# Expert stage: y stores, bias loads and weight-centring transfers moved from SyncE's queue to ScalarE's, token-order tables by matmul

## The chip, the cores and the metric

One Trainium2 chip, one program on its 8 cores, each core with one of the 8 batch rows of x (2048 tokens of 1024 values). Nothing is exchanged between cores. The metric is the device time of the slowest core in microseconds. Each core has TensorE (PE), VectorE (DVE), ScalarE (ACT), GpSimd (POOL) and SyncE (SP, which only issues transfers); 16 DMA engines per core carry what SP, ACT or POOL issue.

## The reference

Two layers, each with an attention-like block and a feed-forward block, every block followed by `x = layernorm(x + block(x))`:

```
L0_attn: state = tanh(state @ A.T + u_t @ B.T) + sp_t ; out = (state @ C.T) @ Wo.T + bo     (a scan)
L0_ffn:  8 experts, the 2 best per token:
         logits = x @ gate_w.T + gate_b ; probs = softmax(logits) ; top 2
         out = sum over the 2 of  prob_e * ( relu(x @ w1[e] + b1[e]) @ w2[e] + b2[e] )
         w1[e]: 1024 x 4096, w2[e]: 4096 x 1024
L1_attn: q, k, v = x @ Wq.T, x @ Wk.T, x @ Wv.T ; 16 heads of 64 ; layernorm of q and k per head ; causal attention ; @ Wu.T
L1_ffn:  token shift, r = sigmoid(xr @ W_r.T), k = relu(xk @ W_k.T)^2, out = r * (k @ W_v.T)
```

## The kernel before, in words

The program is written as five instruction lists, one per engine. Helpers (`MM`, `AC`, `DV`, `GP`, `DMA`, `E`) append an instruction with the semaphore values that it waits for, and `run` issues each list in order. So **each engine's order is the order of the Python code**, a wait at the head of an engine's list holds everything behind it, and in the profile nearly every instruction has the line of `run`, L1431 (the gathers have L1416). Groups are told apart by tile names.

Stages: the scan (0 to about 215 us); routing, in which each token's normed row `x1b` is scattered in bf16 to the rows `xg_d` (`xgs`) of its two experts by POOL's indirect transfers (`scatter`); the experts; the gathering of the two results of each token (`fetch`, `combine`); queries, keys and values; attention; the last feed-forward block.

**Routing.** `route` computes for each of 16 tiles of 128 rows the target row of each row's two copies, `posU`, and `ends` computes the gate values, `gate`. Both are in the scan's order: row 32k+s is position k of the 64-token run s. After the experts the tokens are wanted in their own order, so `posN` and `gateN` hold the same numbers with the rows permuted: partition 64h+k of tile i is position k of run 2i+h. Before, they are made by storing `posU` and `gate` to DRAM (`po_d`, `ga_d`: `to_table`) and reading them back with another access pattern (`of_table`), rows of 8 bytes each.

**Experts.** Each of the 8 experts has a fixed capacity of 640 rows. `load_xg(e)` is one transposing transfer (`dma_start_transpose`) of 640 x 1024 bf16 from `xg_d` into `xgT[e % 2]`. `mlp` then runs:

- first product: 32 blocks `hb` of 128 hidden units, each 8 x 2 matmuls of 128x320 into PSUM banks 0 and 1 or 2 and 3; ACT's Relu with bias turns each block into `hT`.
- second product: 5 tiles `s` of 128 rows, each 32 x 2 matmuls of 128x512 into banks 4 and 5 (even s) or 6 and 7 (odd s); DVE adds the bias row `b2r` into `yst[s % 2]`, which frees the two banks; then `yst` is stored to `yb_d` (`ybs`). A tile s needs the banks that tile s-2 used, so TensorE can run two tiles ahead of DVE's sum.

Weights come by POOL's queue in 32 casting transfers per expert (f32 in DRAM, bf16 in SBUF): `load_w1(e+1, c)` when the first product of expert e has used chunk c, `load_w2(e+1, c)` when the last tile of its second product has.

The loop over experts also hides a job for layer 1: the centring of Wq and Wk in 32 pieces, 4 per expert. `center_load(j)` loads a piece into the single buffer `wqf`, `center_run(j)` lets DVE take the mean of each 64 columns off (`wsum`, `wqc`) and stores it to `wc_d` (`wcs`).

Before, all of these are in SP's queue, in this order for expert e: the transposing load of e+1 (its wait is the end of the first product of e-1); during the first product at blocks 0, 8, 16, 24 a `center_load` and at 4, 12, 20, 28 a `center_run` with its store; at block 1 `load_b2(e)` (which waits for the last sum of e-1); then the five y stores. The loads of the centred weights `WqS`, `WkS`, of `cb2` and of `x1c` follow behind the last expert.

Of the kernel before, what the change touches and what calls it, by code (L numbers as in the profile page):

```python
# [13 lines left out]
T = 2048  # L14
D = 1024
NE = 8
# [16 lines left out]
def build():  # L33
    nc = bass.Bass("TRN2", target_bir_lowering=False)

    def din(name, shape, dtype=F32):
        return nc.dram_tensor(name, list(shape), dtype, kind="ExternalInput").ap()
# [8 lines left out]
    bo_d = din("bo", [1, D])  # L46
    cf_d = din("cf", [128, 310])
    cg_d = din("cg", [128, 80])
    cb_d = din("cb", [128, 640], BF16)
    lnrow_d = din("lnrow", [1, 256])  # L50
    w1_d = din("w1", [NE, 16, 128, 2048])
# [12 lines left out]
    rc_d = scratch("rcs", [16, T], F32)  # L64
    lo_d = scratch("los", [1, T], F32)
    ao_d = scratch("aos", [8, 128, T], BF16)
    po_d = scratch("pos", [T, 2], U32)
    ga_d = scratch("gas", [T, 2], F32)
    bl_d = scratch("bls", [2, D], BF16)

    base = (nc.sbuf_base + 63) & ~63
# [57 lines left out]
    bib = place("bib", [128, 512], BF16, OY + 6912)  # L129
    b3 = place("b3", [3, D], BF16, OB)  # L130
    xgE = [place(f"xgE{i}", [8, 512], F32, (OB + 2048, OF + 26624)[i]) for i in range(2)]
    sz = place("sz", [128, NTILE], F32, OB + 7424)
    WiF = place("WiF", [128, D], F32, O1)
    WsF = place("WsF", [128, 8, 128], F32, O1 + 4096)
# [87 lines left out]
    def V(s):  # L222
        return (side[0] + s, cnt.get(side[0] + s, 0))
# [34 lines left out]
    t_bo = DMA("sync", "lbo", bo1[0], bo_d)  # L258
    DMA("sync", "lc", cf, cf_d)
    DMA("sync", "lc", cg, cg_d)  # L260
    t_lc = V("lc")
    gwT, boT, I8 = cg[:, 0:64].rearrange("p (c e) -> p c e", c=8), cg[:, 64:72], cg[0:8, 72:80]
    DMA("sync", "lw", BTf, BT_d)
# [194 lines left out]
    def post(S, nx):  # L458
# [94 lines left out]
        def route(nt):  # L553

            i0, n = 4 * nt, 4
            bank = 6 + nt % 2
            ts = slice(i0, i0 + n)
            L, o0, o1, M = LG[:, ts], ohs[0][:, ts], ohs[1][:, ts], Mall[:, ts]
            a, b, c, d = (tm[j][:, 0:n] for j in range(4))
            mx = tm[4][:, 0:n]  # L560
            v1, v2, vA, vB = (tv[j][:, 0:n] for j in range(4))

            def ex(x):
                return x.unsqueeze(2).broadcast_to([128, n, NE])

            def al(x):
                return x.unsqueeze(1).broadcast_to([128, n, NE])

            t = DV("tensor_tensor", a, ex(mv[:, ts, 0]), al(SgB), ALU.mult, w=(st["sg"], S.get("rt")))
            t = DV("tensor_tensor", b, ps[:, bank, 0:8 * n].rearrange("p (i e) -> p i e", e=NE), a,  # L570
                   ALU.subtract, w=(t, S["lg", nt]))
            t = DV("tensor_tensor", c, b, ex(rs[:, ts]), ALU.mult, w=(t, S["rs", i0 + n - 1]))
            t = DV("tensor_tensor", L, c, al(gbr), ALU.add, w=(t,))
            for i in range(n):
                t = DV("max", mx[:, i, :], L[:, i, :], w=(t,))
            DV("tensor_copy", MX[:, ts], mx[:, :, 0], w=(t,))
            t = DV("tensor_tensor", a, L, mx[:, :, 0:1].broadcast_to([128, n, NE]), ALU.is_equal)
            t = DV("tensor_tensor", b, a, al(rev8), ALU.mult, w=(t,))
            t = DV("tensor_reduce", v1, b, AX.X, ALU.max, w=(t,))
            t = DV("tensor_tensor", c, al(rev8), ex(v1), ALU.is_equal, w=(t,))  # L580
            t = DV("scalar_tensor_tensor", d, c, -1e30, L, ALU.mult, ALU.add, w=(t,))
            t = DV("tensor_tensor", a, d, mx[:, :, 1:2].broadcast_to([128, n, NE]), ALU.is_equal, w=(t,))
            t = DV("tensor_tensor", b, a, al(rev8), ALU.mult, w=(t,))
            t = DV("tensor_reduce", v2, b, AX.X, ALU.max, w=(t,))
            DV("tensor_tensor", vA, v1, v2, ALU.max, w=(t,))
            t = DV("tensor_tensor", vB, v1, v2, ALU.min)
            DV("tensor_tensor", o0, al(rev8), ex(vA), ALU.is_equal, w=(t,))
            t = DV("tensor_tensor", o1, al(rev8), ex(vB), ALU.is_equal)
            t = DV("tensor_tensor", M, o0, o1, ALU.add, w=(t,))
            for i in range(i0, i0 + n):  # L590
                t = DV("tensor_tensor", Mc[:, i + 1, :], Mc[:, i, :], Mall[:, i, :], ALU.add, w=(t,))
            S["mc"] = t
            r = ps[:, bank, 256:256 + 8 * n]
            MM(r, Lst, M.rearrange("p i e -> p (i e)"), start=True, stop=False, w=(t, t_cb))
            t = MM(r, ones_b, Mc[:, ts].rearrange("p i e -> p (i e)"), start=False, stop=True, inc=True)
            r = r.rearrange("p (i e) -> p i e", e=NE)
            t0 = DV("tensor_tensor", a, r, al(eoff), ALU.add, w=(t,))
            t = S["rf", nt] = DV("scalar_tensor_tensor", b, r, float(CAP), al(kadd), ALU.is_ge, ALU.mult)
            t = DV("tensor_tensor", c, a, b, ALU.add, w=(t,))
            for k, o in enumerate((o0, o1)):  # L600
                t = DV("tensor_tensor", a, c, o, ALU.mult, w=(t,))
                t = DV("tensor_reduce", (v1, v2)[k], a, AX.X, ALU.add, w=(t,))
                t = DV("tensor_copy", posU[:, ts, k], (v1, v2)[k], w=(t,))
            S["rt"] = S["pos"] = t

        def scatter(i):
# [7 lines left out]
        def ends():  # L614
# [10 lines left out]
            for k in range(2):  # L625
                t1 = DV("tensor_tensor", ge[2], ge[1], ohs[k], ALU.mult, w=(t,))
                t1 = DV("tensor_reduce", gs[0], ge[2], AX.X, ALU.add, w=(t1,))
                t = S["gate"] = DV("tensor_tensor", gate[:, :, k], gs[0], gs[1], ALU.mult, w=(t1,))

        return load_x, tile_z, tile_all, tile_n, gate_x, gate_y, route, scatter, ends  # L630

# [106 lines left out]
    t_scat = tuple(st["scg", g] for g in range(4))  # L738
    t_x1all = tuple(st["x1s", i] for i in range(10, NTILE))
    t_vscan, t_pscan, t_gscan, t_ascan = V("v"), V("p"), V("g"), V("a")  # L740
    t_gate, t_fl = st["gate"], st["fl"]

    tk = {("a", 0): t_vscan, ("a", 2): t_ascan, ("y", 4): t_gate}
# [1 line left out]
    def mlp(e, row0, nst, xsrc, tx, tk, t_w1, t_w2):  # L746
# [16 lines left out]
        for s in range(nst):  # L763
            bk = 4 + 2 * (s % 2)
            for kb in range(32):
# [5 lines left out]
                if s == nst - 1 and kb % 2 == 1:  # L771
# [3 lines left out]
            tk["y", bk] = DV("tensor_tensor", yb, ps[:, bk:bk + 2, :], b2r, ALU.add,  # L775
                             w=(t, tk["b2", e], tk.get(("ys", s % 2))))
            tk["yv", e] = tk["y", bk]
            tk["ys", s % 2] = DMA("sync", f"sy{s % 2}", yb_d[row0 + s * 128:row0 + (s + 1) * 128, :], yb,
                                  w=(tk["y", bk],))
            yield ("y", s)  # L780

    def load_b2(e, w=()):
        tk["b2", e] = DMA("sync", "b2", b2r, b2_d[e:e + 1, :].partition_broadcast(128), w=w)

    x1p = x1_d.rearrange("(s k) d -> k s d", k=NSEG)

# [7 lines left out]
    for c in range(8, 16):  # L794
# [2 lines left out]
    tk["ys", 0] = t_zf  # L797

    to_table = [(d.rearrange("(i p) c -> p i c", p=128), o) for d, o in ((po_d, posU), (ga_d, gate))]  # L800
    of_table = [(o[64 * h:64 * h + 64], d.rearrange("(s i h) c -> h s i c", i=NTILE, h=2)[h]) for h in range(2)
                for d, o in ((po_d, posN), (ga_d, gateN))]

    with only_if(flag[0:1, 0:1], t_fl, "x"):
        X = chain()
        for o, i in to_table + of_table:
            X("sync", "dma_start", out=o, in_=i)
        rest = xg_d[MAIN:ROWS, :].rearrange("(a p r) d -> a p (r d)", p=128, r=2)
        fill = hT[:, 0:4, :].rearrange("p a b -> p (a b)")[:, 0:2048]  # L810
        X("vector", "memset", fill, 0.0)
# [34 lines left out]
    def center_load(j):  # L846
        m, k, h = j // 16, j // 2 % 8, j % 2
        src = (WqT_d, WkT_d)[m]
        st["wl", j] = DMA("sync", "wl", wqf, src[k * 128:(k + 1) * 128, h * 512:(h + 1) * 512],
                          w=(st.get(("wc", j - 1)), t_vscan, t_gate, t_pscan))  # L850

    def center_run(j):
# [4 lines left out]
        t = DV("tensor_tensor", wqc.rearrange("p (h s) -> p h s", s=64), v,  # L857
               wsum.unsqueeze(2).broadcast_to([128, 8, 64]), ALU.subtract, w=(t, st.get(("ws", j - 1))))
        st["wc", j] = t
        st["ws", j] = DMA("sync", "ws", wc_d[m, k * 128:(k + 1) * 128, h * 512:(h + 1) * 512], wqc, w=(t,))  # L860

    for e in range(NE):
        if e + 1 < NE:
            load_xg(e + 1, w=(tk.get(("m1", e - 1, 31)),))
        for ev, j in mlp(e, e * CAP, CAP // 128, xgT[e % 2], tk["xg", e], tk, t_w1, t_w2):
            if ev == "m2" and e == 0 and j == 0:
                for o, i in to_table:
                    DMA("sync", "tab", o, i, w=(t_gate,))
                t_tab = V("tab")
            if ev == "m1" and e == 1 and j == 8:  # L870
                for o, i in of_table:
                    t_pos = DMA("sync", "tab", o, i, w=(t_tab,))
            if ev == "m1" and j % 8 == 0:
                center_load(4 * e + j // 8)
            if ev == "m1" and j % 8 == 4:
                center_run(4 * e + j // 8)
            if ev == "m1" and j == 1 and e > 0:
                load_b2(e, w=(tk["yv", e - 1],))
            if ev == "m1" and j % 2 == 1 and e + 1 < NE:
                load_w1(e + 1, j // 2, w=(tk["m1", e, j],))  # L880
            if ev == "m2" and e + 1 < NE:
                load_w2(e + 1, j, w=(tk["m2", e, j],))
# [577 lines left out]
def _prep(i):  # L1460
# [18 lines left out]
    for j, k in enumerate(("qln_w", "qln_b", "kln_w", "kln_b")):  # L1479
# [7 lines left out]
    cf[:, 294:302] = MAIN - CAP + e * (T - 2 * CAP)  # L1487
    cf[:, 302:310] = A("L0_ffn_gate_b")
    d["cf"] = cf
    d["cg"] = C(np.concatenate([A("L0_ffn_gate_w").reshape(8, 8, 128).transpose(2, 1, 0).reshape(128, 64),  # L1490
                                A("L0_attn_bo").reshape(8, 128).T, np.eye(128, 8, dtype=np.float32)], 1))
    d["lnrow"] = C(np.concatenate([A("L1_attn_" + k) for k in ("qln_w", "qln_b", "kln_w", "kln_b")]).reshape(1, 256))
# [32 lines left out]
```

How the kernel before makes its waits and increments, by code:

```python
    def run(eng, lst):  # L1402
        for method, args, kw, need, s, n in lst:
            plain = method in HELD or method in ("wait_", "if_", "gather_")
            for sn, v in need if plain else need[:-1]:
                eng.wait_ge(sems[sn], v)
            if method == "wait_":
                continue
            if method == "gather_":
# [4 lines left out]
                        for c in calls:  # L1414
                            call = {k: v for k, v in c.items() if k != "sem"}
                            eng.indirect_dma_start(**call).then_inc(sems[c["sem"][0]], 16)
                continue
# [5 lines left out]
            if method == "held_":  # L1423
                out, weights, rhs = args
                ins = eng.add_instruction(mybir.InstMatmult(
                    name=nc.get_next_instruction_name(), engine=mybir.EngineType.PE, start_tensor_calc=False,
                    stop_tensor_calc=True, tile_size=(128, 128), tile_position=(0, 0), ldweights=False,
                    bass_skip_group_check=True, ins=(eng.lower_ap(rhs), eng.lower_ap(weights)),
                    outs=(eng.lower_ap(out),)))
            else:
                ins = getattr(eng, method)(*args, **kw)
            if need and not plain:
                ins._wait_ge(sems[need[-1][0]], need[-1][1])
            if s is not None:
                ins.then_inc(sems[s], n)
```

## Time and profile before

| | |
|---|---|
| median of 3 runs | 2644.66 us (2635.55 to 2655.49) |
| the profiled execution: its own time | 2658.42 us |
| its span on core 6, the slowest | 2656.8 us |
| spans of the 8 cores | 2628.6 to 2656.8 us |
| granted TensorE clock, mean of each core | 0.883 to 0.889 |
| TensorE busy | 1989.0 us (75%) |
| DMA | 304.33 MB moved, mean 115 GB/s |

The span runs from the first to the last instruction of a core; the time beside it is 1.6 us longer. A granted clock of 1.00 is 2.4 GHz, 0.50 is 1.2 GHz. SPq is SP as issuer of transfers: its duration is that of the issue, not of the transfer. Times of rows are in us from the span's start unless marked ns.

### The profile page before, as it was taken

To read this page: it belongs to the slowest core of one execution; us is meant where nothing else is said; L and a number is where in the kernel's file an instruction comes from. 1 tells how busy PE (TensorE), PEld (TensorE's weight loads), DVE (VectorE), ACT (ScalarE), POOL (GpSimd) and SP (SyncE) were. 2 spreads that over 40 slices of the span, in tenths; PEclk is the share of its full clock that TensorE was granted. 3 is DMA by queue.
4 is the path that set the end of the run, shared out by engine and by line. 5 is a ranking of instruction groups with operands and counts; after the bars stand their busy time and mean duration, and the time that the engine had idled before them with its cause. 6 is when DMAs were issued, how large, how long until landed. Compare 5 with 4: busy or idle time off the path is not lost.

```text
span 2656.8 us, 25477 instructions; the slowest of 8 cores (2628.6 to 2656.8 us)
## 1 busy us (share of the span) xinstructions
PE 1989.0 (75%) x10425; PEld 999.1 (38%) x10537; DVE 692.7 (26%) x1350; ACT 808.8 (30%) x1159; POOL 439.7 (17%) x484
## 2 busy tenths in 40 slices
PE   5653939919969599696996992778788778566766
PEld 2112615605527255272562741333233223232332
DVE  4541010010010100101001102663344344355454
ACT  2222201201203012030120300456678778333222
POOL 1124101001011010010100002210123232112133
PEclk9666969959979799797997996999989999788988
DMA  9677976977939769397693826750001411611100
GB/s 273 226 184 178 167 138 85 128 132 125 164 93 169 139 117 170 89 168 146 116 168 89 155 64 195 212 164 9 2 17 25 86 27 25 131 36 56 40 32 40
DMA packets 143494, 304.33 MB, mean 115 GB/s; under 512 B 63984, under 2 KB 69873, under 8 KB 141300
## 3 DMA queue, kind: packets, MB, share of 16 engines
q0 software_dynamic: 49296, 169.90, 37.9%
q1 hardware_dynamic: 94052, 132.51, 18.3%
q8 instruction: 89, 1.46, 0.2%
q14 instruction: 57, 0.47, 0.1%
HBM read 367.08 MB, written 69.37 MB: 164 GB/s over the span
## 4 chain that ended last, share of the span: by engine, by line
SPq 28%; PE 26%; issue 12%; DVE 12%; ACT 11%; DMA 7%; POOL 4%; DVEq 0%; POOLq 0%; ACTq 0%; another core or an unknown queue 0%
SPq L1431 28%; PE ps L1431 26%; ACT PT L1431 5%; DMA wqf<-WqT 3%; ACT rsd L1431 2%; DVE PT L1431 2%; DMA wqf<-WkT 2%; POOL x3f L1431 1%; DVE lstf L1431 1%; DVE wsum L1431 1%; DMA sumC<-stg 1%; ACT sq L1431 1%; DVE xk L1431 1%; DVE rf L1431 1%; DVE xt L1431 1%
## 5 line engine op out<-in xcount | busy, mean ns | idle before, releaser
L1431 PE MATMUL ps<-W,hT 128*128 128x512 bf16 x2504 | 566.1, 387 | 233.9 <-DVE yst L1431 231.0
L1431 PE MATMUL ps<-xgT,W 128*128 128x320 bf16 x4096 | 559.9, 300 | 30.6 <-DMA xgT<-xgs 30.1
L1431 ACT ACTIVATE hT<-ps,cf 128x640 bf16<-128x640 f32 x256 | 203.0, 793 | 1081.9 <-PE ps L1431 1081.9
L1431 PEld LDWEIGHTS ps<-xgT,W 128*128 128x128 bf16 x4096 | 401.4, 98 | 188.7 <-issue 30.2
L1431 PEld LDWEIGHTS ps<-W,hT 128*128 128x128 bf16 x2560 | 253.6, 99 | 545.1 <-DVE yst L1431 234.4
L1431 POOL DMA_DIRECT2D W<-w x256 | 135.6, 537 | 1103.4 <-PE ps L1431 1049.1
L1431 ACT ACTIVATE PT<-ps 128x1024 bf16<-128x1024 f32 (+7 forms) x384 | 272.0, 793 | 82.2 <-PE ps L1431 79.3
L1431 DVE TENSOR_REDUCE wsum<-wqf 128x8 f32<-128x512 f32 x32 | 21.9, 686 | 921.6 <-DMA wqf<-WqT 535.1
L1431 PE MATMUL ps<-PT,Vg 128*128 128x512 bf16 (+3 forms) x628 | 191.9, 365 | 58.1 <-DVE PT L1431 56.6
L1431 PE MATMUL ps<-qz,KT 128*128 128x512 bf16 (+3 forms) x627 | 186.9, 364 | 19.1 <-POOL qz L1431 12.4
L1431 DVE TENSOR_TENSOR PT<-PT,cb 128x128 bf16<-128x128 bf16 x256 | 111.6, 456 | 177.3 <-ACT PT L1431 174.4
L1431 DVE TENSOR_TENSOR yst<-ps,b2r 128x1024 f32<-128x1024 f32 x40 | 48.3, 1222 | 362.8 <-PE ps L1431 362.8
L1431 PEld LDWEIGHTS ps<-PT,Vg 128*128 128x128 bf16 x640 | 65.1, 102 | 143.1 <-DVE PT L1431 92.2
L1431 POOL TENSOR_TENSOR aoT<-stg,recB 64x2048 bf16<-64x2048 f32 x15 | 67.6, 4506 | 194.8 <-DMA recB<-rcs 194.8
L1431 PEld LDWEIGHTS ps<-qz,KT 128*128 128x128 bf16 x640 | 51.1, 101 | 110.5 <-ACT PT L1431 76.9
L1431 PE MATMUL ps<-Wu,aoT 128*128 128x512 bf16 x249 | 67.3, 429 | 30.4 <-DVE aoT L1431 18.6
L1431 PE MATMUL ps<-WvS,x2T 128*128 128x512 bf16 x249 | 64.8, 416 | 32.7 <-ACT x2T L1431 32.4
L1431 PE MATMUL ps<-xk,Wkf 128*128 128x512 bf16 x250 | 60.9, 402 | 14.4 <-DVE xk L1431 14.0
L1431 PE MATMUL ps<-Wr,xr 128*128 128x512 bf16 x249 | 58.9, 387 | 14.8 <-DVE xr L1431 8.7
L1431 PE MATMUL ps<-x2T,WqS 128*128 128x512 bf16 x250 | 62.8, 383 | 0.4 <-issue 0.2
L1431 POOL TENSOR_TENSOR x3f<-x3f,rf 128x1024 f32<-128x1024 f32 x16 | 37.5, 2342 | 140.7 <-DVE rf L1431 140.7
L1431 PE MATMUL ps<-x2T,WkS 128*128 128x512 bf16 x251 | 60.2, 379 | 0.7 <-ACT sq L1431 0.5
(208 smaller groups left out, 1578.6 us busy)
## 6 DMA issues: line engine op xcount, KB each, us to landing
W<-w POOLq DMA_DIRECT2D x256, 512.0 KB, 39.3
ybs<-yst SPq DMA_DIRECT2D x40, 512.0 KB, 2.8
xgs<-zero SPq DMA_DIRECT2D x20, 512.0 KB, 17.1
xTf<-xT SPq DMA_DIRECT2D x8, 1024.0 KB, 18.1
xt<-x SPq DMA_DIRECT2D x16, 512.0 KB, 8.7
x1s<-xt SPq DMA_DIRECT2D x16, 512.0 KB, 5.0
x1c<-x1s SPq DMA_DIRECT2D x32, 256.0 KB, 7.7
x2s<-x1c SPq DMA_DIRECT2D x16, 512.0 KB, 2.9
```

Source lines behind the costliest of these rows:

```text
L1431: ins = getattr(eng, method)(*args, **kw)
```

## The change

In the expert loop SP's queue keeps only the transposing loads. The y stores, the bias loads and both transfers of each centring piece go to ACT's queue. The centring is no longer spread over the first product: at the event behind tile s of the second product comes `center_run` of the piece before (s > 0), then `center_load` of the next (s < 4), and behind tile 4 the bias load of the next expert. The tables `posN` and `gateN` are no longer sent through DRAM: `posU`'s values are kept in f32 (`posF`), DVE multiplies them and `gate` with a mask into `perm` (four operations, 128x128 each), four f32 matmuls with a constant `peye` (16 columns) put them in token order, and three small DVE operations write `posN` and `gateN`. A constant `cp` of 128 x 24 f32 is loaded at the start of SP's queue.

```diff
+    t_cp = DMA("sync", "lcp", cp, cp_d)
...
-                t = DV("tensor_reduce", (v1, v2)[k], a, AX.X, ALU.add, w=(t,))
-                t = DV("tensor_copy", posU[:, ts, k], (v1, v2)[k], w=(t,))
+                t = DV("tensor_reduce", posF[:, ts, k], a, AX.X, ALU.add, w=(t,))
+                t = DV("tensor_copy", posU[:, ts, k], posF[:, ts, k], w=(t,))
...
+            for v, src in enumerate((posF[:, :, 0], posF[:, :, 1], gate[:, :, 0], gate[:, :, 1])):
+                t = DV("tensor_tensor", perm[:, v].rearrange("p (h i r) -> p h i r", h=2, r=4),
+                       pmask.rearrange("p (h r) -> p h r", h=2).unsqueeze(2).broadcast_to([128, 2, NTILE, 4]),
+                       src.unsqueeze(1).unsqueeze(3).broadcast_to([128, 2, NTILE, 4]), ALU.mult, w=(t, t_cp))
+            for v in range(4):
+                t1 = MM(ps[:, 7, 192 + 16 * v:208 + 16 * v], perm[:, v], peye, start=True, stop=True, w=(t,),
+                        inc=(v == 3))
+            r = ps[:, 7, 192:256].rearrange("p (v i) -> p i v", v=4)
+            t = DV("tensor_scalar", ge[2][:, :, 0:2], r[:, :, 0:2], 0.25, None, ALU.add, w=(t1,))
+            t = DV("tensor_copy", posN, ge[2][:, :, 0:2], w=(t,))
+            S["posn"] = DV("tensor_copy", gateN, r[:, :, 2:4], w=(t,))
...
-            tk["ys", s % 2] = DMA("sync", f"sy{s % 2}", yb_d[row0 + s * 128:row0 + (s + 1) * 128, :], yb,
+            tk["ys", s % 2] = DMA("scalar", f"sy{s % 2}", yb_d[row0 + s * 128:row0 + (s + 1) * 128, :], yb,
...
-        tk["b2", e] = DMA("sync", "b2", b2r, b2_d[e:e + 1, :].partition_broadcast(128), w=w)
+        tk["b2", e] = DMA("scalar", "b2", b2r, b2_d[e:e + 1, :].partition_broadcast(128), w=w)
...
-        st["wl", j] = DMA("sync", "wl", wqf, src[k * 128:(k + 1) * 128, h * 512:(h + 1) * 512],
+        st["wl", j] = DMA("scalar", "wl", wqf, src[k * 128:(k + 1) * 128, h * 512:(h + 1) * 512],
...
-        st["ws", j] = DMA("sync", "ws", wc_d[m, k * 128:(k + 1) * 128, h * 512:(h + 1) * 512], wqc, w=(t,))
+        st["ws", j] = DMA("scalar", "ws", wc_d[m, k * 128:(k + 1) * 128, h * 512:(h + 1) * 512], wqc, w=(t,))
...
-            if ev == "m2" and e == 0 and j == 0:
-                for o, i in to_table:
-                    DMA("sync", "tab", o, i, w=(t_gate,))
-                t_tab = V("tab")
-            if ev == "m1" and e == 1 and j == 8:
-                for o, i in of_table:
-                    t_pos = DMA("sync", "tab", o, i, w=(t_tab,))
-            if ev == "m1" and j % 8 == 0:
-                center_load(4 * e + j // 8)
-            if ev == "m1" and j % 8 == 4:
-                center_run(4 * e + j // 8)
-            if ev == "m1" and j == 1 and e > 0:
-                load_b2(e, w=(tk["yv", e - 1],))
+            if ev == "y":
+                if j > 0:
+                    center_run(4 * e + j - 1)
+                if j < 4:
+                    center_load(4 * e + j)
+                elif e + 1 < NE:
+                    load_b2(e + 1, w=(tk["yv", e],))
```

## Rows read from the trace of the kernel before

**Rows 1.** The page: shares of the chain that ended last, by line.
```profile
SPq L1431 28%; PE ps L1431 26%; ACT PT L1431 5%; DMA wqf<-WqT 3%; ACT rsd L1431 2%; DVE PT L1431 2%; DMA wqf<-WkT 2%; POOL x3f L1431 1%; DVE lstf L1431 1%; DVE wsum L1431 1%; DMA sumC<-stg 1%; ACT sq L1431 1%; DVE xk L1431 1%; DVE rf L1431 1%; DVE xt L1431 1%
```

**Rows 2.** The page: the second product; busy, mean ns, idle before, releaser.
```profile
L1431 PE MATMUL ps<-W,hT 128*128 128x512 bf16 x2504 | 566.1, 387 | 233.9 <-DVE yst L1431 231.0
```

**Rows 3.** Timeline of PE, 380 to 1620 us: start, length, idle before and releaser.
```profile
391.02 44.01 PE L1431 MATMUL ps<-W,hT 128*128 128x512 bf16 x188 [46.08 <-DVE yst L1431]
...
586.44 43.58 PE L1431 MATMUL ps<-W,hT 128*128 128x512 bf16 x188 [54.24 <-DVE yst L1431]
629.85 69.71 PE L1431 MATMUL ps<-xgT,W 128*128 128x320 bf16 x512
...
753.66 43.59 PE L1431 MATMUL ps<-W,hT 128*128 128x512 bf16 x188 [26.47 <-DVE yst L1431]
...
1535.15 69.02 PE L1431 MATMUL ps<-W,hT 128*128 128x512 bf16 x313
```

**Rows 4.** Timeline of SP's queue, 230 to 800 us: start, length of the issue.
```profile
236.69 6.00 SPq L1431 DMA_TRANSPOSE xgT<-xgs  x1
...
423.46 18.32 SPq L1431 DMA_DIRECT2D gas<-gate  x1
441.88 58.00 SPq L1431 DMA_DIRECT2D ybs<-yst  x1
500.01 61.41 SPq L1431 DMA_TRANSPOSE xgT<-xgs  x1
...
631.83 98.63 SPq L1431 DMA_TRANSPOSE xgT<-xgs  x1
...
731.14 0.67 SPq L1431 DMA_DIRECT2D b2r<-b  x1
...
737.41 0.33 SPq L1431 DMA_DIRECT2D wcs<-wqc  x1
```

**Rows 5.** Timeline of DVE, 590 to 800 us.
```profile
630.12 1.23 DVE L1431 TENSOR_TENSOR yst<-ps,b2r 128x1024 f32<-128x1024 f32 x1 [12.59 <-PE ps L1431]
...
735.65 0.69 DVE L1431 TENSOR_REDUCE wsum<-wqf 128x8 f32<-128x512 f32 x1 [104.30 <-DMA wqf<-WqT]
...
736.64 0.69 DVE L1431 TENSOR_TENSOR wqc<-wqf,wsum 128x512 bf16<-128x512 f32 x1
...
752.39 2.35 DVE L1431 TENSOR_TENSOR yst<-ps,b2r 128x1024 f32<-128x1024 f32 x2
```

**Rows 6.** Busy time by stretch: PE, PEld, DVE, ACT, POOL, granted clock, DMA share, GB/s.
```profile
753.00:757.00 4.00, 3.34 (x8) 1.19 (x9) 1.73 (x2) 0.00 (x0) 0.00 (x0) 0.50 0.73 290
...
629.00:797.00 168.00, 141.16 (x830) 82.19 (x836) 12.13 (x17) 25.41 (x32) 16.71 (x32) 0.92 0.79 137
...
1421.00:1605.00 184.00, 182.33 (x1013) 100.74 (x1024) 16.83 (x22) 25.38 (x32) 10.12 (x18) 0.98 0.47 95
```

**Rows 7.** DMA, 700 to 797 us: busy tenths in 40 slices, transfers by median us to landing.
```profile
DMA  9999999999999991314050650000031000058999
...
wqf<-WqT SPq DMA_DIRECT2D x4, 256.0 KB, 2.9
...
wcs<-wqc SPq DMA_DIRECT2D x4, 128.0 KB, 1.8
```

**Rows 8.** The same of 629 to 700 us: weights and the transposing load in flight.
```profile
ybs<-yst SPq DMA_DIRECT2D x1, 512.0 KB, 9.2
```

**Rows 9.** Timeline from the last expert to layer 1, all engines.
```profile
1606.06 0.38 SPq L1431 DMA_DIRECT2D WqS<-wcs  x1
...
1635.68 1.28 DVE L1431 SCALAR_TENSOR_TENSOR x1c<-yA,gateN,x1c 128x1024 f32<-128x1024 f32 x1 [30.18 <-DMA x1c<-x1s]
```

**Rows 10.** Timeline of the start, and of the end of routing.
```profile
1.89 0.42 SPq L1431 DMA_DIRECT2D cg<-cg  x1
...
219.23 0.18 DVE L1431 TENSOR_TENSOR gate<-gs,gs 128x16 f32<-128x16 f32 x1
...
233.45 0.96 POOL L1431 DMA_INDIRECT xgs<-x1b,posU  x1 [0.30 <-issue]
```

More of the change, by code:

```diff
@@ L48, in build @@
     cg_d = din("cg", [128, 80])
+    cp_d = din("cp", [128, 24])
     cb_d = din("cb", [128, 640], BF16)
@@ L66, in build @@
     ao_d = scratch("aos", [8, 128, T], BF16)
-    po_d = scratch("pos", [T, 2], U32)
-    ga_d = scratch("gas", [T, 2], F32)
     bl_d = scratch("bls", [2, D], BF16)
@@ L131, in build @@
     xgE = [place(f"xgE{i}", [8, 512], F32, (OB + 2048, OF + 26624)[i]) for i in range(2)]
+    cp = place("cp", [128, 24], F32, OB + 7488)
+    posF = place("posF", [128, NTILE, 2], F32, OB + 7584)
+    perm = place("perm", [128, 4, 128], F32, OF + 4096)
     sz = place("sz", [128, NTILE], F32, OB + 7424)
@@ L260, in build @@
     DMA("sync", "lc", cg, cg_d)
+    t_cp = DMA("sync", "lcp", cp, cp_d)
+    pmask, peye = cp[:, 0:8], cp[:, 8:24]
     t_lc = V("lc")
@@ L740, in build @@
     t_vscan, t_pscan, t_gscan, t_ascan = V("v"), V("p"), V("g"), V("a")
-    t_gate, t_fl = st["gate"], st["fl"]
+    t_gate, t_fl, t_pos = st["gate"], st["fl"], st["posn"]
     tk = {("a", 0): t_vscan, ("a", 2): t_ascan, ("y", 4): t_gate}
@@ L797, in build @@
     tk["ys", 0] = t_zf
-    to_table = [(d.rearrange("(i p) c -> p i c", p=128), o) for d, o in ((po_d, posU), (ga_d, gate))]
-    of_table = [(o[64 * h:64 * h + 64], d.rearrange("(s i h) c -> h s i c", i=NTILE, h=2)[h]) for h in range(2)
-                for d, o in ((po_d, posN), (ga_d, gateN))]
     with only_if(flag[0:1, 0:1], t_fl, "x"):
         X = chain()
-        for o, i in to_table + of_table:
-            X("sync", "dma_start", out=o, in_=i)
         rest = xg_d[MAIN:ROWS, :].rearrange("(a p r) d -> a p (r d)", p=128, r=2)
@@ L1489, in _prep @@
     d["cf"] = cf
+    q = np.arange(128)[:, None]
+    j = np.arange(16)[None]
+    d["cp"] = C(np.concatenate([(q % 2 == j[:, :8] // 4) & (q // 32 == j[:, :8] % 4), q % 32 // 2 == j], 1), np.float32)
     d["cg"] = C(np.concatenate([A("L0_ffn_gate_w").reshape(8, 8, 128).transpose(2, 1, 0).reshape(128, 64),
```

## The prediction

> **What bounds the kernel now.** I read the page's chain first: 28% of the span is SP's queue as issuer [rows 1], an engine that computes nothing. The page's group of the second product says whom it holds: TensorE is idle for 231.0 us before these matmuls, all put down to DVE's `yst` [rows 2]. PE's timeline shows where. The second product of an expert runs two of its five tiles, then stands still, then runs the other three: 46.08 us in expert 0, 54.24 in expert 1, 26.47 in expert 2 [rows 3], and four more of 24.63 to 26.95 in experts 3 to 6. Expert 7 has none: its 320 matmuls take 69.02 us in one piece [rows 3].
>
> SP's timeline gives the reason. The transposing load for expert 3 is issued at 631.83, behind the last y store of expert 1, and its issue alone takes 98.63 us; behind it in the same queue stand a centring piece and the bias row of expert 2, issued at 731.14 [rows 4]. DVE, in order too, waited 104.30 us for the first piece, then did four pieces with a load's latency between each, and only at 752.39 came to the two sums that free the PSUM banks [rows 5]; PE resumes at 753.66. In expert 1 the same queue was blocked once more, by the tables: storing `gate` in rows of 8 bytes took 18.32 us to issue and the y store behind it 58.00, so that the transposing load began at 500.01 [rows 4].
>
> Each stall costs something after its end too. The granted clock is 0.50 (1.2 GHz) in the 4 us after the restart, following 26 us without matmuls [rows 6]. Three tiles without a stall are 3/5 of 69.02 = 41.4 us; the restarted three of expert 2 plus start of the next product are 43.4 us (I take start to start). Over the seven restarts these pieces add to 305.4 us from PE's timeline, of which the first, second and third have their rows [rows 3], against 7 x 41.4 = 289.9: 15.5 us.
>
> **The stalls removed.** With the transposing loads alone in SP's queue, nothing that DVE's sums need stands behind them. Removed: 231.0 + 15.5 = 246.5 us. Check from the other side: from the start of expert 0's second product (317.4) to the end of expert 7's (1604.2) are 1286.8 us; eight second products of 69.02 and seven first ones of 69.76 are 1040.5; the difference is 246.3.
>
> **What is late next.** Three things could take the place of the wait.
>
> The transposing load. That of e+1 may now be issued when the first product of e-1 ends, and is needed 209 us later; its longest issue so far is 98.63 us, so it is covered twice. It should also be shorter: the first was issued in 6.00 us, before the weights started [rows 4]. Expert 0 is special: its load for expert 1 is issued at 249 and landed about 370 (121 us, the longest of the eight); the first product of expert 1 will now begin at 317.4 + 69 = 386.4. That leaves 16 us.
>
> The weights. The period of an expert falls from 167 us to 69.7 + 69.0 = 139 us, and the mean DMA share in it is 0.79 of 168 us [rows 6], which is 133 us of full DMA time. So DMA will be at 95%. It still fits: the burst begins with the last tile (616.9 for this period), and the row of slices falls from 9 to 1 at about 741 [rows 7], after 124 us, with everything that was queued moved; it includes the transposing load, whose bytes do not grow. The stall lies in the slack behind that and takes it from 44 us to 17. What the burst brings last is wanted a further product later, so a few us of lateness cost nothing; only a mean over 139 us would. I put 0 here, at most 8 us in each of 6 periods (50).
>
> ACT's queue. ACT now has the waits. In the second product it has no eviction to do, so a store that waits for DVE there delays nobody. At the end it does: behind the last store stand the store of the centring piece and the next bias load, and behind these the Relu of block 0 of the next expert, which PE needs before block 2, 4.36 us after its start. Counted from PE's start at 629.85: the sum ends at 631.35, the piece's DVE work takes 1.68 (735.65 to the end of `wqc` at 737.33), so its store can be issued at 633.1, with 0.33 for it and 0.43 to 0.67 for the bias row, by SP's rows [rows 4, 5]; then the Relu, 0.79, ends at 634.9 and PE, which wanted it at 634.2, starts at about 635.0. That is 0.8 us, times 7 experts: **+5.6 us**. No row has ACT issuing a transfer; if it takes up to 1.3 us each instead of 0.4, three of them add 2.7 us per expert. So 4 to 25 us, and I stay near the lower end because SP's direct rows are the nearest.
>
> **The transfers themselves.** They meet weights and a transposing load now. A y store landed after 9.2 us in that company [rows 8]; a piece's load took 2.9 [rows 7]. With two `yst` buffers a store has some 26 us, and a piece's load some 11 us before DVE comes to it after the next sum (tiles come every 13.8 us). Even at 9.2 both are in time: 0. The bias row has 80 us.
>
> **The end of the experts.** Before, `WqS` was issued at 1606.06, right behind the last store, and the first `x1c` came behind it; DVE waited for that until 1635.68 [rows 9]. `WqS` needs the store of piece 31, which now is issued only after the last sum: sum ends 1605.5, DVE 1.7, issue 0.4, landing 1.8 [rows 7], so 1609.3. **+3.2 us**, taken in full since the whole chain behind moves with it; 0 to 4.
>
> **The tables.** Routing ends for DVE at 219.23; POOL's last scatter starts at 233.45 and the transposing load waits for it [rows 10]. Four operations of 0.3 us (128x128 f32, as that on `ge`), four f32 matmuls under 0.6 us, three small ones with hand-overs are some 4 us, beside POOL's 14: 0. If that cover were gone they would cost these 4. The extra constant is one more issue ahead of the loads of x: **+0.4 us** [rows 10].
>
> **The sum.** 246.5 - 5.6 - 3.2 - 0.4 = 237.3 us less. Against the profiled execution's own time, 2658.4, that gives 2421; it lay 13.8 us above the median of the runs shown, so against the median 2644.66 - 237.3 = **2407 us**. The seven other cores had 217.5 to 229.9 us of these waits, so the slowest core may gain a little less or be another; 10 us for that.
>
> **A rule that speaks against it.** The rows say that an issue can take 98.63 us when the queue is backed up [rows 4]. The Trainium skill, DMA: Bandwidth & Descriptors, section Issuing engines are not separate DMA queues, holds that all issuers share the same 16 engines and that several of them save only the sequencer's time, "usually small relative to the DMA itself". By it the gain would be some tenths of a us per store and the time unchanged; here the sequencer's time is what TensorE waits for, so I give it to the rival below that gains nothing.
>
> **The rivals.**
>
> A. ACT's stores are held up while SP issues a transposing load, for instance in something that both share; in the steady state that load then competes with weights only until some 40 us into the second product and ends there, just when the third sum wants its buffer, so it costs almost nothing. In experts 0 and 1 it does cost: the load for expert 2 follows at 346 right behind the one for expert 1 and lasts some 97 us, into expert 0's fifth tile at 373: about 75 us. Time 2480. For it: 58.00 us for one y store behind an 8-byte one [rows 4] shows that a queue can back up. Against: it was its own queue. 9%.
>
> B. The other side. As A, but the load keeps its 98 us in every expert, from the end of the first product. The third sum waits for the first store, PE stops at the fifth tile, 55 us into the product, until 98 plus some 5 us of landing and sum: 48 us, plus 2.2 of half clock, seven times 351 us in place of the 246.5. Time 2407 + 351 = 2758. It decides from a hold of 82 us on: 82 + 5 - 55 is a stall of 32 us, which with its 2.2 eats the whole 237.3 in seven experts. Against: nothing but weights slowed that load, and these have drained 124 us after the burst's start, which is 40 us into the second product. 4%.
>
> C. The weights become the bound: 5 to 10 us more in six periods, 2440 to 2465. For: 95% DMA. 8%.
>
> D. Nothing is gained since another wait takes over in full (a centring piece that lands late in front of each sum): about 2645. Pieces take 2.9 us alone, so it would need five times that under load. 3%.
>
> E. Unbroken work costs clock. Every 1% less over the 1110 us of the stage is 11 us; from a mean of 0.82 on the gain is gone. Against: 184 us with one short gap ran at 0.98 [rows 6]. The Trainium skill, TensorE: Matmul & The Clock Gate, Part 1, names a limiter that holds a die at 13/16 under dense matmuls on three or more cores; no row shows that here, with eight cores dense. By its figure, as an estimate, 256 us come back: 2663. 4%.
>
> **Chances.** My forecast 72%, A 9, B 4, C 8, D 3, E 4. Below it there is only the spread of the runs, 10 us, and a smaller cost at ACT: 2385. Above, C lies inside and A is the edge: 2485. A measurement here tells about 1% (26 us) from no change. Faster by over 1%: forecast, A and C, 89%, and half of E, 91%. Within 1%: D and half of E, 5%. Slower: B, 4%.
>
> **What would show it.** In the profile after: second products of 320 matmuls in one piece of 69 us, expert period 139 to 140 us; no PE wait on `yst`; a wait of 0.8 us on `hT` in front of block 2 of each expert; transposing issues well under 98 us from expert 3 on; DMA share about 0.95 in an expert; DVE's wait for `x1c` ending some 245 us earlier than 1635.68. I am wrong if ACT's issues of y stores are longer than 1 us, if POOL's weights or the first product wait on `W` or `xgT`, or if the granted clock of 400 to 1300 us is under 0.98.

## The result and the profile after

The changed kernel takes 2511.18 us (median of 4 runs; 2642.99 for the kernel before beside it). The ratio is **0.9473**, interval 0.9422 to 0.9523: faster, but by 139 us where 237 were forecast, and outside the range of 2385 to 2485 that I gave. Here and below, a run in which the cores of one die ran at a lower clock (of the four here, that of 2656 us) is left out of the ratio but not of the median, which is why the ratio isn't quite the quotient of the two medians. In the profiled execution (2509.64 us) the cores are no longer alike: their spans run from 2422.3 to 2508.0 us.

The page of the slowest core, core 7: the two products; the columns are those of [rows 2]:

```profile
L1434 PE MATMUL ps<-xgT,W 128*128 128x320 bf16 x4096 | 570.1, 303 | 118.1 <-ACT hT L1434 95.7
L1434 PE MATMUL ps<-W,hT 128*128 128x512 bf16 x2560 | 553.8, 379 | 0.0
```

The 231.0 us of idle time in front of the second product [rows 2] are 0.0. In their place stand 95.7 us in front of the first product, released by ACT's `hT`. PE's timeline on the same core, to be held against [rows 3]:

```profile
315.20 69.23 PE L1434 MATMUL ps<-W,hT 128*128 128x512 bf16 x320
384.26 4.51 PE L1434 MATMUL ps<-xgT,W 128*128 128x320 bf16 x32
468.15 67.43 PE L1434 MATMUL ps<-xgT,W 128*128 128x320 bf16 x480 [79.37 <-ACT hT L1434]
535.42 69.23 PE L1434 MATMUL ps<-W,hT 128*128 128x512 bf16 x320
604.48 4.51 PE L1434 MATMUL ps<-xgT,W 128*128 128x320 bf16 x32
609.79 65.37 PE L1434 MATMUL ps<-xgT,W 128*128 128x320 bf16 x480 [0.80 <-ACT hT L1434]
...
1174.64 4.51 PE L1434 MATMUL ps<-xgT,W 128*128 128x320 bf16 x32
1184.20 67.80 PE L1434 MATMUL ps<-xgT,W 128*128 128x320 bf16 x480 [5.05 <-ACT hT L1434]
```

Each second product runs in one piece. But the first product now stops after 32 matmuls, which are two blocks, and waits for the first Relu: 79.37 us in expert 1, then 0.80, 3.34, 2.62, 3.23, 5.05 and 1.34. The 480 matmuls behind take up to 67.80 us instead of 65.37 when the wait was long, the half clock again (9.5 us over the seven). The stage from expert 0's second product to expert 7's end lasts 1461.2 - 315.2 = 1146.0 us; 1286.8 before, 1040.5 without any wait.

What ACT did in these 79 us, in its own timeline (ACTq is ACT as issuer of transfers):

```profile
384.76 0.33 ACTq L1434 DMA_DIRECT2D wcs<-wqc  x1
385.11 0.45 ACTq L1434 DMA_DIRECT2D wqf<-WqT  x1
386.18 0.33 ACTq L1434 DMA_DIRECT2D ybs<-yst  x1
466.44 0.33 ACTq L1434 DMA_DIRECT2D wcs<-wqc  x1
466.80 0.45 ACTq L1434 DMA_DIRECT2D b2r<-b  x1
467.30 1.48 ACT L1434 ACTIVATE hT<-ps,cf 128x640 bf16<-128x640 f32 x2 [151.10 <-DVE wqc L1434]
```

And DVE:

```profile
464.68 0.69 DVE L1434 TENSOR_REDUCE wsum<-wqf 128x8 f32<-128x512 f32 x1 [78.86 <-DMA wqf<-WqT]
```

So the chain is: the load of the fourth centring piece, issued at 385.11, lands at 464.6, 79.5 us later; DVE waits for it; ACT waits for DVE with the piece's store at the head of its queue; the first Relu stands behind. The issues themselves are as short as SP's, 0.33 to 0.45 us.

The DMA view says what else was in flight. First 329 to 384 us, then 441 to 466 us of the same core; columns: packets, MB, share of 16 engines' time. q0 carries the weights, q1 what SP issues (here only transposing loads), q10 what ACT issues:

```profile
q0 software_dynamic: 1910, 6.96, 74.8%
q10 hardware_dynamic: 1278, 3.08, 18.5%
q1 hardware_dynamic: 2024, 0.51, 11.2%
```

```profile
q1 hardware_dynamic: 1066, 0.27, 136.5%
q0 software_dynamic: 104, 0.38, 8.4%
q10 hardware_dynamic: 64, 0.15, 3.4%
```

In the first stretch one packet of the transposing load takes 0.112 x 16 x 55 us / 2024 = 0.05 us. In the second it takes 1.365 x 16 x 25 / 1066 = 0.51 us, ten times as long, although the weights are nearly through; hardly anything else moves, ACT's packets included. But these are only the last 25 of the 79 us. In 408 to 440 us, with the piece's load issued and PE standing, q10 moves nothing at all:

```profile
q0 software_dynamic: 1351, 4.90, 81.1%
q1 hardware_dynamic: 1913, 0.49, 35.2%
```

Here weights run at 4.90 MB in 32 us, 153 GB/s, and a transposing packet takes 0.352 x 16 x 32 / 1913 = 0.09 us. So the slow packets are how the wait ends and not what it is made of; what holds ACT's packets in the 32 us before them the trace doesn't show. The transposing load in flight is that for expert 2: an issue of 115.80 us and 143.1 us to landing.

```profile
L1434 SPq DMA_TRANSPOSE xgT<-xgs x1: 115796/115796/115796, 337.6 to 337.6; - x1
...
DMA to landing us min/median/max: 143.1/143.1/143.1
```

The wait at expert 1 is 69.0, 39.2, 5.6, 57.6, 26.5, 8.4, 7.8 and 79.4 us on cores 0 to 7. Three cores (2, 5 and 6) wait 5.6 to 8.4 us only, and their spans, 2430.3, 2422.3 and 2440.8 us, are within 20 us of the 2421 of my sum. Core 4 waits 26.5 us although its transposing packets take no more than 0.05 us then (380 to 411 us: 1070 packets, 10.1%).

In the later experts the same chain is shorter. ACT at expert 5 of core 7:

```profile
1121.38 0.45 ACTq L1434 DMA_DIRECT2D wqf<-WkT  x1
1134.77 0.33 ACTq L1434 DMA_DIRECT2D ybs<-yst  x1
1153.87 0.33 ACTq L1434 DMA_DIRECT2D wcs<-wqc  x1
...
1182.33 0.33 ACTq L1434 DMA_DIRECT2D wcs<-wqc  x1
1182.68 0.62 ACTq L1434 DMA_DIRECT2D b2r<-b  x1
1183.35 1.48 ACT L1434 ACTIVATE hT<-ps,cf 128x640 bf16<-128x640 f32 x2 [76.78 <-issue]
```

The first piece's load, issued at 1121.38, holds its store back to 1153.87, 32 us; the other three catch up, but the fourth is stored at 1182.33, when PE had wanted the Relu at 1179.0.

### The profile page after: what moved, and what is told of

The parts are those of the page before. It is cut to its first block, busy times and chain, and to the rows that moved or that the text cites. A ratio compares the mean times of both kernels' runs of the same rounds, so it can differ in the third digit from the quotient of the medians.

```text
span 2508.0 us, 25623 instructions; the slowest of 8 cores (2422.3 to 2508.0 us)
## 1 busy us (share of the span) xinstructions
PE 1992.9 (79%) x10564; PEld 999.9 (40%) x10545; DVE 700.5 (28%) x1357; ACT 807.5 (32%) x1159; POOL 439.5 (18%) x484
## 4 chain that ended last, share of the span: by engine, by line
PE 51%; DVE 11%; ACT 11%; issue 9%; DMA 8%; POOL 4%; another core or an unknown queue 3%; SPq 0%; ACTq 0%; POOLq 0%; DVEq 0%
PE ps L1434 50%; ACT PT L1434 5%; DMA wqf<-WkT 3%; DMA wqf<-WqT 3%; DVE PT L1434 3%; ACT rsd L1434 3%; POOL x3f L1434 2%; DVE lstf L1434 1%; ACT sq L1434 1%; DVE xk L1434 1%; DVE rf L1434 1%; DVE xt L1434 1%; DMA xTf<-xT 1%; DVE lsmf L1434 1%
## 5 line engine op out<-in xcount | busy, mean ns | idle before, releaser
L1434 PE MATMUL ps<-xgT,W 128*128 128x320 bf16 x4096 | 570.1, 303 | 118.1 <-ACT hT L1434 95.7
L1434 PE MATMUL ps<-W,hT 128*128 128x512 bf16 x2560 | 553.8, 379 | 0.0
```

What stands on the lines that cost most here:

```text
L1434: ins = getattr(eng, method)(*args, **kw)
```

## The experiments

Where expert 1's wait is called long below, it is over 20 us. **Theory A**: the transposing load for expert 2, in flight beside ACT's transfers, holds them. **Theory B**: DMA is overloaded by weights at that place. Beside both: the fourth centring piece, ahead of the first Relu, is what turns a late transfer into idle TensorE. All ratios are against the kernel before on the same chip.

**1. The transposing loads one expert later.**

```diff
-        if e + 1 < NE:
-            load_xg(e + 1, w=(tk.get(("m1", e - 1, 31)),))
+        if e == 0:
+            load_xg(1)
...
+            if ev == "m1" and j == 31 and 0 < e < NE - 1:
+                load_xg(e + 1, w=(tk["m1", e, 31],))
```

> The changed kernel with the transposing loads of experts 2 to 7 issued one expert later (at the end of the first product of the expert before, not of the one before that), so that expert 0's second product has only the load for expert 1 beside it. Theory A (the ACT queue's transfers are held by the transposing load for expert 2, which starts right behind the one for expert 1 while weights are queued): TensorE's wait on hT at the start of expert 1 (5.6 to 79.4 us by core) falls below 10 us on every core, time 2425 to 2450. Theory B (DMA is simply overloaded by weights there): the wait stays at 40 us or more on the slowest cores, time 2490 to 2515.

Measured: 2465.73 us, ratio 0.9252 (0.9192 to 0.9312). The wait at expert 1 is 3.5 to 12.4 us over the eight cores. That is 0.022 of the time, 58 us of 2643, gained by moving one transfer. The worst waits are a little above the 10 us expected, and on four cores (0, 2, 5 and 6) waits of 2 to 5 us stay from expert 3 on. PE on core 0:

```profile
405.48 68.23 PE L1436 MATMUL ps<-xgT,W 128*128 128x320 bf16 x480 [10.67 <-ACT hT L1436]
548.36 65.37 PE L1436 MATMUL ps<-xgT,W 128*128 128x320 bf16 x480 [1.23 <-ACT hT L1436]
```

**2. The fourth piece later.** Its `center_run` at block 30 of the next expert's first product.

```diff
-                if j > 0:
+                if 0 < j < 4 or (j == 4 and e == NE - 1):
                     center_run(4 * e + j - 1)
...
+            if ev == "m1" and j == 30 and e > 0:
+                center_run(4 * e - 1)
```

> The changed kernel with the fourth centring piece of each expert worked on and stored at block 30 of the next expert's first product, so that between the last tile and the first Relu ACT has only a y store and the bias load. If the wait is that of ACT for DVE and of DVE for the piece's load: the wait on hT falls to 0 to 1 us in every expert, all cores, time 2415 to 2435. If ACT's own issues are what is held up: the wait of 79 us stays on the slowest core, time about 2510.

Measured: 2483.01 us, 0.9288 (0.9213 to 0.9363). Five cores show no wait on `hT` in any expert, with spans of 2403.5 to 2416.0 us. On the other three the slow stretch comes at other places: core 1 waits 82.51 us at expert 2, and on cores 3 and 4 PE stands still for 31.4 and 10.2 us inside expert 1's first product, with no releaser shown, and then waits on `W` some seven times for 0.8 to 2.6 us. Core 1:

```profile
615.53 4.71 PE L1436 MATMUL ps<-xgT,W 128*128 128x320 bf16 x24 [82.51 <-ACT hT L1436]
```

In expert 1's second product core 3 stands for another 22.8 us and core 4 for 8.3 us, and on core 1 a piece's load took 91.5 us to land. The five cores without a wait show that the fourth piece is what PE waits for in the changed kernel; the other three, that taking it out of the way doesn't take away what holds the transfers, it only moves the victim. A miss of both sizes expected.

**3. Each half alone.** `tables_alone` is the kernel before with the tables by matmul; `queues_alone` is the changed kernel with the tables through DRAM, whose diff is the table part of the change taken back.

> The kernel before with the tables by matmul and nothing else of the change. Expert 1's stall falls from 54.2 to that of the other experts, 26.5, and no other changes: 28 us less, time about 2615. Rival: the time in which the table stores delayed the transposing load is filled by it, no gain, 2643.

Measured: 2633.07 us, 0.985 (0.9758 to 0.9941), 40 us less with an interval of 16 to 65; the 28 expected lie inside. Expert 1's stall falls to that of the others, as expected; PE on core 4:

```profile
390.94 43.55 PE L1435 MATMUL ps<-W,hT 128*128 128x512 bf16 x188 [46.27 <-DVE yst L1435]
557.81 22.37 PE L1435 MATMUL ps<-W,hT 128*128 128x512 bf16 x91 [26.15 <-DVE yst L1435]
```

> The changed kernel with the tables through DRAM as before, in SP's queue. The table stores now stand between the transposing loads for experts 1 and 2. Theory A: what is in flight beside ACT's transfers at the end of expert 0 is then the store of the tables in 8 byte rows; if these hold ACT's transfers as the transposing load does, the wait at expert 1 is 40 to 80 us again, time 2500; if only a transposing load does it, the wait is under 10 us and the time 2440. Theory B: as the changed kernel, 2510.

Measured: 2558.78 us, 0.9555 (0.9472 to 0.9638), the time of neither theory. The waits at expert 1 are 9.6 to 20.0 us, but a new one comes that neither theory had: the table stores delay the transposing load for expert 2 until PE wants it. Core 0:

```profile
607.51 6.27 PE L1432 MATMUL ps<-xgT,W 128*128 128x320 bf16 x32 [72.19 <-DMA xgT<-xgs]
```

On cores 3, 4 and 7 there are also waits of 21.9 to 28.7 us on `hT` or `yst` in expert 2. By themselves the queues give 0.045 and the tables 0.015 of the time, together 0.053: most of the gain is the queues' part.

**4. Is it the transposing, the small packets, or the bytes?** `load_plain` loads the same bytes without transposing; `load_small` cuts them into as many pieces of 256 bytes as the transposing load has. The edit of `load_small`; that of `load_plain` has one piece of 10 KB per partition instead:

```diff
-        tk["xg", e] = E("sync", "dma_start_transpose", out=xgT[e % 2], in_=xg_d[e * CAP:(e + 1) * CAP, :],
+        tk["xg", e] = E("sync", "dma_start", out=xgT[e % 2].rearrange("p c (a d) -> p c a d", a=5),
+                        in_=xg_d[e * CAP:(e + 1) * CAP, :].rearrange("(a p) (c d) -> p c a d", p=128, c=8),
```

> The changed kernel with plain loads of the same bytes in place of the transposing ones (xgT then holds the rows in another order, so the experts compute on other numbers; all else is the same). Theory A (the transposing load holds the others): waits on hT under 3 us everywhere, time 0.915 of before. Theory B (too much DMA): waits of 40 to 80 us stay at expert 1 on the slowest cores, 0.947.

Measured: 2455.68 us, 0.921 (0.9134 to 0.9286). The wait at expert 1 is 4.9 to 10.2 us, in later experts 0.4 to 4.8.

> As load_plain, but the plain load is cut into 5120 pieces of 256 bytes per expert, the packet size and number of the transposing one. If small packets that take turns with weights are what fills the queues: the same slow stretch as in the changed kernel, waits of 40 to 80 us on the slowest cores. If it is the transposing itself: as load_plain.

Measured: 2461.99 us, 0.9234 (0.9158 to 0.931). The wait at expert 1 is 4.0 to 11.4 us. The worst core of each, 7 and 4:

```profile
397.19 68.07 PE L1435 MATMUL ps<-xgT,W 128*128 128x320 bf16 x480 [10.22 <-ACT hT L1435]
```

```profile
404.30 67.75 PE L1435 MATMUL ps<-xgT,W 128*128 128x320 bf16 x480 [11.43 <-ACT hT L1435]
```

No core of the two profiles has a long wait, though the bytes are the same: theory B falls. Small packets alone weren't seen to make one either. The two kernels also separate issue from landing. The issue of the load for expert 2 took 0.3 us plain, 0.6 us in small pieces and 37 to 133 us transposing; it landed after some 12 us plain, 138 to 145 us on six cores and 63 to 64 on two in small pieces, and 71 to 148 us transposing. So the packets' number and size account for the late landing, and only the transposing goes with the long issue. But short issues also put expert 1's load ahead of the weights (issued at 238 to 247, landed 7 to 22 us later), so these kernels differ from the changed one in two things, and the fair comparison is experiment 5, where one transposing load is left beside the weights: 2 of 8 cores there, none of 16 here. That speaks for the transposing, but with so few cores it is not proof. What I had expected too low is what stays: 4 to 11 us at expert 1 and up to 4.8 us later come from the piece, transposing or not.

**5. Two transposing loads in a row, or one?** `t1_first` issues the load for expert 1 right behind the first, ahead of the weights, and leaves that for expert 2 in place. `after_again` is the changed kernel on the same chip.

```diff
     load_xg(0, w=t_x1all)
+    load_xg(1)
     for c in range(4, 16):
-        load_w1(0, c, w=t_x1all + (t_vscan, t_gscan, tk["xg", 0]) + t_scat)
+        load_w1(0, c, w=t_x1all + (t_vscan, t_gscan, tk["xg", 0], tk["xg", 1]) + t_scat)
     for c in range(8, 16):
-        load_w2(0, c, w=(t_pscan, tk["xg", 0]))
+        load_w2(0, c, w=(t_pscan, tk["xg", 0], tk["xg", 1]))
```

> The changed kernel with only the transposing load for expert 1 moved ahead of the weights; that for expert 2 stays where it is, at the end of expert 0's first product, beside ACT's transfers. If one transposing load beside weights and ACT's transfers is enough for the slow stretch: waits on hT of 20 to 80 us at expert 1 on some cores, time 0.945 of before. If it takes two of them in a row, the second issued while the first still drains: under 12 us on all cores, 0.925.

Measured: 2500.47 and 2502.95 us, 0.939 of 2663.37; two times are too few for an interval. Cores 0 and 7 wait 67.1 and 60.4 us at expert 1, the other six 7.4 to 17.1.

```profile
455.18 67.57 PE L1436 MATMUL ps<-xgT,W 128*128 128x320 bf16 x480 [67.08 <-ACT hT L1436]
```

Core 7 in 406 to 438 us, while PE waits:

```profile
q0 software_dynamic: 1269, 4.60, 85.1%
q1 hardware_dynamic: 1673, 0.43, 24.4%
q10 hardware_dynamic: 52, 0.15, 3.3%
```

A transposing packet takes 0.244 x 16 x 32 / 1673 = 0.07 us: there is a long wait without the packets of 0.51 us.

> The changed kernel itself once more, on the chip of t1_first, to see whether the long wait at expert 1 comes back and on which cores: theory A, 20 to 80 us on two to five of the eight cores, not the same ones as before (cores 0, 1, 3, 4 and 7), 0.947.

Measured: 2524.57 us, 0.9471 (0.9422 to 0.952). Waits at expert 1 of 49.9, 7.9, 66.2, 71.8, 83.0, 23.5, 31.5 and 69.0 us. Over 20 us on seven cores, five in the first profile, and not always the same. So one transposing load is enough for a long wait; two in a row had it on more cores in these three profiles.

**6. Both edits, and with the second load first.** `both_moved` has the edits of 1 and 2; `two_first` has that of 5 in addition.

> The changed kernel with both edits: the transposing loads of experts 2 to 7 one expert later, and the fourth centring piece finished in the next expert's first product. No transposing load but the first is then beside expert 0's second product, and nothing but a store and a bias load is ahead of the Relu: waits on hT of 0 to 1 us in all experts and cores, 0.915 of the kernel before. If a transposing load beside ACT's transfers does harm in the later experts too, waits of 10 us and more come back there at random on some cores, 0.925 to 0.93.

Measured: 2423.51 us, 0.909 (0.9032 to 0.9147); once more on another chip (`both_again`) 2427.58 us, 0.9094 (0.9039 to 0.9149):

> both_moved once more, on the chip of one_queue: no long wait on any core, 0.909.

No core waits on `hT`. The page of the slowest core:

```profile
L1438 PE MATMUL ps<-xgT,W 128*128 128x320 bf16 x4096 | 559.2, 299 | 23.5 <-DMA xgT<-xgs 23.5
L1438 PE MATMUL ps<-W,hT 128*128 128x512 bf16 x2560 | 553.8, 379 | 0.0
```

The eight spans lie between 2402.9 and 2420.7 us. Against experiment 1 the piece is worth another 0.016, 43 us. Taken in the other order the piece gives 49 us (experiment 2) and the load 52 us; each of the four differences is uncertain by some 20 us. In these versions, and in that of experiment 1, the six later transposing loads are also issued at the start of a second product, beside ACT's transfers, with issues of 26 to 55 us, and none goes with a long wait. So a transposing load beside ACT's transfers isn't enough for one; why expert 0's second product is the place stays open.

> As both_moved, and the transposing load for expert 1 is issued right behind the first, before the weights of expert 0 (which wait for it). Alone it should take about 6 us instead of some 97, and nothing waits for these weights before 262 us. Waits on hT of 0 to 1 us, no wait for xgT at expert 1, 0.910 of the kernel before. If weights start too late: TensorE waits on W in expert 0's first product, up to 6 us.

Measured: 2424.04 us, 0.9093 (0.9036 to 0.915). The second load takes 6.9 us to issue and 10.6 to land on core 0, in place of 92.6 and 130.6 in `both_moved`, and changes nothing: what it was spared was hidden.

**7. The order alone, in one queue.** `two_first` with every `"scalar"` of the change put back to `"sync"`:

```diff
-            tk["ys", s % 2] = DMA("scalar", f"sy{s % 2}", ...
+            tk["ys", s % 2] = DMA("sync", f"sy{s % 2}", ...
```

> The order of two_first, but everything back in SP's queue: y stores, bias loads, centring. It asks whether the second queue is needed or only the order. A transposing load then begins at the end of each first product, ahead of that expert's y stores, and nothing of ACT's is beside it; weights drain some 40 us into the second product, so the first y store can go at about 45 us and the third sum at 48, before the fifth tile starts at 55. If so: no wait on yst or hT, 0.91 of before. If the load keeps some 97 us: stalls of 40 us and more on yst in each expert, 1.0 or slower.

Measured: 2422.41 us, **0.9077** (0.9038 to 0.9115), no wait on `yst` in any expert. SP's queue of core 7 at expert 1:

```profile
457.75 39.30 SPq L1437 DMA_TRANSPOSE xgT<-xgs  x1
497.14 1.10 SPq L1437 DMA_DIRECT2D ybs<-yst  x1
498.29 0.42 SPq L1437 DMA_DIRECT2D wqf<-WqT  x1
498.81 1.20 SPq L1437 DMA_DIRECT2D ybs<-yst  x1
```

The transposing load blocks the queue for 39.30 us, the first y store goes 39 us into the second product, and the third sum still finds its buffer before the fifth tile needs its banks. So a second queue isn't needed for this time. The order that gives it differs from the kernel before in three things, though: the place of the transposing load, that of the centring, and the tables. Which share the load's place alone would have in one queue no run shows. The versions of 6 and 7 all beat both kernels and can't be told from each other.

## Why the prediction was wrong

**The stalls removed, 246.5 us: right.** Second products of 69.23 us in one piece, no wait on `yst`; with the two edits of experiment 6 the ratio is 0.909, my forecast 2407/2644.66 is 0.910.

**The step that failed: "ACT's queue ... +5.6 us"**, 0.8 us for each expert. It measured 95.8 us of waits plus 9.5 us of half clock on the slowest core. I took for its inputs the short issues, and these were right (0.33 to 0.45 us), but counted the piece's DVE work as starting right behind the last sum. That rests on the step under "The transfers themselves", where I put 0: a piece's load landed in 2.9 us alone, a y store in 9.2 us beside weights and a transposing load, and I took 9.2 as the most for either, against 11 us of room. Both halves were wrong. The 9.2 us were of a store issued just ahead of the transposing load. Of a transfer issued behind one, with the transposing load and weights in flight, the trace of before did have rows, and I priced none: the first piece's load, on core 6 issued at 346.14, landed 25.3 us later (24.1 to 28.1 on the eight cores), beside a transposing load that took 121.3 us to land.

```profile
wqf<-WqT SPq DMA_DIRECT2D x1, 256.0 KB, 25.3
```

That is more than the 11 us of room; by this row the Relu is late at expert 1. The 79.5 us of the changed kernel it doesn't foretell. And in the window of the fourth piece the weights' burst starts, so that without a long wait, too, the piece's load lands after 12 to 15 us (experiment 1), and PE waits up to 11 us at expert 1 and 5 later even with plain loads (experiment 4).

**The two parts of the miss**, by the runs: the transposing load for expert 2 beside expert 0's second product, 58 us (experiment 1); the piece ahead of the Relu, 43 us (experiment 6 against 1). Together 101 us, against the 98 missing; that they fit so closely is partly luck, given the intervals.

**Rival A** named the place, the load for expert 2 beside expert 0's tiles, and 75 us, at 9%. The path was another (the fourth piece's load and the Relu, not the third sum's buffer), and the size differs by core, from 5.6 to 83.0 us; the slowest core decides. I gave it too little, since I argued from rows of one queue about what two do to each other. That ACT's transfers are held while SP issues is not shown either: later loads with issues of up to 55 us went with no long wait (experiment 6). And I took it as alone, when the piece adds to it. Rival B did not come: the five transposing issues of core 7 behind that for expert 2 take 17 to 39 us. Rival C did not come; DMA's share in an expert is 0.90 on core 7 in 535 to 675 us (0.82 to 0.97 over cores and experts), in `both_moved` even 0.99 without any wait on weights. Rival D no. Rival E no: the granted clock is 0.98 to 1.00 on all cores in 535 to 1400 us. My sign for it, under 0.98 in 400 to 1300 us, did show on core 7 (0.95), but by the stall at expert 1, where it was 0.50 in 397 to 466 us with PE idle; in `both_moved` it is 1.00.

**The end of the experts, +3.2**: PE's gap before layer 1 is 41.75 us against 38.74, +3.0. `WqS` is issued 13 us after the last matmul and not the 5 of my forecast. One small DVE operation of the piece took 5.05 us while a memset of POOL ran; whether that is the reason was not tested. `x1c` landed sooner after it, 21.5 us against 29.6. **The tables, 0**: right, the eight matmul passes take 1.89 us at 219.62, under the scatter. That the table stores held SP's queue in expert 1 was right (experiment 3).

## What to carry to other kernels

A transfer that lands in 3 us in the rows has that time only in that company; before moving it beside another kind, price it from a row where both are in flight, or treat it as unknown; look through the whole trace for such a row, here there was one of 25.3 us. A queue owner that also computes must have nothing in its queue, between its last wait and its next computation, that waits on a load. When a long issue blocks a queue, first ask whether it can be issued at another moment; here that, with the centring moved and the tables by matmul, gave 0.9077 without a second queue.

## What the runs showed of the hardware

A transposing load of 640 x 1024 bf16 took 4 to 9 us to issue ahead of the weights, and landed within 7 to 13 us. The load for expert 1 took 89 to 103 us to issue where weights followed it, most later ones of the kernel before 92 to 99, that for expert 2 in the changed kernel 37 to 133, and in the versions that issue it at the end of the first product (`xg_late`, `both_moved`, `two_first`, `one_queue`) 26 to 55. A plain load of the same bytes took 0.3 us to issue and some 12 us to land, and as 5120 pieces of 256 bytes 0.6 to 2.3 us to issue and, on six of eight cores, 138 to 145 us to land.

With that load for expert 2, weights and ACT's transfers in flight, a load of 256 KB issued by ACT took 79.5 us to land, and for 32 us none of its packets moved. Waits over 20 us for it were seen on 5 and 7 of 8 cores with the changed kernel and on 2 of 8 with only one such load beside the weights (experiment 5); on none of 8 in each profile of `load_plain`, `load_small`, `xg_late`, `both_moved`, `both_again` and `two_first`. They were seen only with a transposing load, weights and another issuer's transfers together, and not every time with these. On core 7 they end in a stretch in which each 256 byte packet of the transposing load takes 0.51 us instead of 0.05, but others come without it. Why some cores have them and others not, and where inside DMA the packets wait, stays open: the trace doesn't tell the 16 engines apart.
